# A gate by ScalarE's Silu in place of a tanh and a VectorE product

## The reference

```
g  = jax.nn.silu(xg @ Wg.T)                  # silu(z) = z * sigmoid(z)
...                                          # out: the recurrence over time
og = ((og - m) / jnp.sqrt(va + 1e-05)).reshape(b, l, e) * gn_w + gn_b
x1 = x + og * g @ Wo.T
...
rr = jax.nn.sigmoid(xr2 @ Wfr.T)
kk = jnp.square(jax.nn.relu(xk2 @ Wfk.T))
return x1 + rr * (kk @ Wfv.T)
```

## Time and profile before

| | value |
|---|---|
| median of three executions | 1783.87 us |
| the profiled execution | 1785.44 us |
| its span, first to last instruction | 1783.7 us |
| TensorE busy | 1718.5 us, 96% |
| VectorE busy | 1638.8 us, 92% |
| ScalarE busy | 1184.9 us, 66% |
| GpSimd busy | 955.0 us, 54% |
| mean granted TensorE clock | 0.984 |
| gate's tanh on ScalarE | 32 times, 22.2 us |
| table loads on ScalarE | 5, 1.28 us each |

### The profile page before, as it was taken

One profiled execution on the slowest core, in us unless ns is written; L12 is line 12 of the kernel. 1 busy time (PEld: TensorE's weight loads), 2 busy tenths in 40 slices (PEclk: granted clock), 3 DMA queues, 4 the chain that ended last, 5 costly groups with the idle time before them and its releaser, 6 DMA issues.

```text
span 1783.7 us, 32768 instructions
## 1 busy us (share of the span) xinstructions
PE 1718.5 (96%) x11408; PEld 1218.0 (68%) x11408; DVE 1638.8 (92%) x2224; ACT 1184.9 (66%) x2954; POOL 955.0 (54%) x752
## 2 busy tenths in 40 slices
PE   5899999999999999999999999999999999999876
PEld 3667677677667677766767776776776676776643
DVE  3599999999999999999999999999999999999982
ACT  4666677676677676667767766776766776776533
POOL 1244556556655755555665566565555566545440
PEclk8999999999999999999999999999999999999988
DMA  6243343343343344434334333334433443433320
GB/s 255 71 108 99 96 104 93 105 116 99 96 103 101 91 113 108 101 92 108 92 100 120 99 100 101 99 94 108 114 100 93 106 99 91 115 93 91 104 68 12
DMA packets 81731, 180.81 MB, mean 101 GB/s; under 512 B 18304, under 2 KB 35072, under 8 KB 80544
## 3 DMA queue, kind: packets, MB, share of 16 engines
q1 hardware_dynamic: 59920, 161.93, 34.9%
q10 hardware_dynamic: 21648, 16.78, 3.0%
HBM read 161.91 MB, written 16.78 MB: 100 GB/s over the span
## 4 chain that ended last, share of the span: by engine, by line
PE 84%; DVE 10%; issue 3%; ACT 1%; POOL 1%; DMA 0%; SPq 0%; DVEq 0%; POOLq 0%; ACTq 0%
PE bank L2011 29%; PE bank L2018 17%; PE bank L2135 6%; PE bank L2043 5%; PE bank L2056 5%; PE bank L2023 5%; PE bank L2092 4%; PE bank L2030 3%; DVE S L873 2%; PE bank L2071 2%; DVE A L885 2%; PE bank L2113 1%; PE bank L2146 1%; DVE A L855 1%; PE bank L2036 1%
## 5 line engine op out<-in xcount | busy, mean ns | idle before, releaser
L855 DVE TENSOR_TENSOR A<-vrep,kt 128x1008 f32<-128x1008 f32 x256 | 310.9, 1224 | 2.4
L560 POOL COPY S<-s 128x16 f32<-128x16 f32 x128 | 81.8, 639 | 409.5 <-DVE A L885 409.4
L873 DVE TENSOR_TENSOR_SCAN S<-wrep,S 128x512 f32<-128x512 f32 x256 | 299.8, 1212 | 1.2 <-issue 0.2
L885 DVE TENSOR_TENSOR A<-S,rt 128x2048 f32<-128x2048 f32 x128 | 291.7, 2279 | 0.1
L534 POOL TENSOR_TENSOR xf<-xf,xa 128x512 f32<-128x512 f32 x160 | 223.1, 1395 | 41.3 <-DVE xf L811 41.1
L1496 ACT ACTIVATE bank<-bank,par 128x128 f32<-128x128 f32 x640 | 173.9, 367 | 39.7 <-PE bank L2092 39.2
L503 POOL TENSOR_TENSOR hrs<-hrs,mhalf 128x32 f32<-128x32 f32 x31 | 176.8, 5704 | 2.6
L501 POOL TENSOR_SCALAR rstd<-mv 128x1 f32<-128x1 f32 (+1 forms) x96 | 84.1, 876 | 161.6 <-DVE mv L748 60.8
L552 POOL TENSOR_TENSOR rk<-rT,kT 128x256 f32<-128x256 f32 x32 | 106.0, 3313 | 103.3 <-DVE oc L910 103.3
L863 DVE TENSOR_TENSOR S<-A 128x1008 f32<-128x1008 f32 x128 | 155.8, 1218 | 0.2
L811 DVE TENSOR_TENSOR xf<-bank,sx 128x512 f32<-128x512 f32 x160 | 108.1, 676 | 44.6 <-PE bank L2011 22.5
(11 more groups left out here) (164 smaller groups left out, 4062.1 us busy)
## 6 DMA issues: line engine op xcount, KB each, us to landing
vrep<-v_dram SPq DMA_DIRECT2D x256, 512.0 KB
xc<-x_c SPq DMA_DIRECT2D x32, 256.0 KB, 6.5
xs<-x_s SPq DMA_DIRECT2D x32, 256.0 KB, 7.3
v_dram<-vT ACTq DMA_DIRECT2D x32, 256.0 KB, 3.1
out<-rr ACTq DMA_DIRECT2D x31, 256.0 KB, 2.8
st<-state SPq DMA_DIRECT2D x64, 2.0 KB, 6.6
Wv<-big_w SPq DMA_DIRECT2D x1, 1024.0 KB, 7.7
Wk<-big_w SPq DMA_DIRECT2D x1, 1024.0 KB, 9.4
```

The lines of the kernel that those rows point to most:

```text
L855: ve_.tensor_tensor(A[:, u % 2, half * WJ:(half + 1) * WJ, 0:P - 2], vrep[:, half, :, 0:P - 2], k, ALU.mult).then_inc(dve_outer.sem, 1)
L873: last = ve_.tensor_tensor_scan(s, w, s, 0.0, ALU.mult, ALU.add)
L885: ve_.tensor_tensor(out4, s, r, ALU.mult).then_inc(dve_read.sem, 1)
```

## The change

ScalarE computes silu(z) from bank G with its own Silu function, and mid_gate is dropped from VectorE's lists at all its places. The factor of a half goes out of gnh. Bank G's reader is now ScalarE's step th, and the last item's tail_gate waits for it.

```diff
-        dve_mid = Steps(sem("dve_mid"), "sx xx mv mw mk mr mg s0m s0c g")
+        dve_mid = Steps(sem("dve_mid"), "sx xx mv mw mk mr mg s0m s0c")
...
-  "G": (dve_mid, "g"),
+  "G": (act_mid, "th"),
...
-                po.tensor_scalar(gnh[:, :, :], gn, 0.5, None, ALU.mult).then_inc(pool_const, 1)
+                po.tensor_copy(gnh[:, :, :], gn).then_inc(pool_const, 1)
...
-            def mid_gate(n, m, p):
-
-                eng.wait_ge(act_mid.sem, act_mid.count("th", n))
-                ve_.scalar_tensor_tensor(gT[:, p, :, :], gT[:, p, :, :], 1.0, by_chunk(bank_of("G")[:, :]),
-                                         ALU.add, ALU.mult).then_inc(dve_mid.sem, 1)
...
                 if n == NB - 1:
-                    eng.wait_ge(dve_mid.sem, dve_mid.count("g", n))
+                    eng.wait_ge(act_mid.sem, act_mid.count("th", n))
...
-                mid_gate(*b2)
...
-                sc.activation(gT[:, p, :, :], by_chunk(bank_of("G")[:, :]), ACT.Tanh, scale=0.5).then_inc(act_mid.sem, 1)
+                sc.activation(gT[:, p, :, :], by_chunk(bank_of("G")[:, :]), ACT.Silu).then_inc(act_mid.sem, 1)
```

More of the change, by code:

```diff
@@ L271, in build @@
                   "Tx": (act_mid, "xa"), "W1": (act_mid, "tn"), "Wt": (act_mid, "tx"), "Vp": (act_mid, "vT"), "D1": (act_mid, "dt"),
-                  "D2": (act_mid, "ez"), "E2": (act_mid, "ez"), "Kp": (act_mid, "k"), "Rp": (act_mid, "r"), "G": (dve_mid, "g"),
+                  "D2": (act_mid, "ez"), "E2": (act_mid, "ez"), "Kp": (act_mid, "k"), "Rp": (act_mid, "r"), "G": (act_mid, "th"),
                   "C": (dve_tail, "o1"), "C2": (dve_tail, "o2"), "Tg": (act_tail, "oT"), "Wo": (dve_tail, "x1"),
@@ L1029, in opening @@
                 att_rstd(*at(2))
-                mid_gate(*at(0))
                 mid_shift(*at(1))
@@ L1076, in opening @@
                 att_aggr(*at(3))
-                mid_gate(*at(1))
                 wkv_outer(*at(1), 1)
@@ L1133, in opening @@
                 mid_s0c(*at(2))
-                mid_gate(*at(2))
                 att_rstd(*at(4))
@@ L1264, in closing @@
                 mid_s0c(*at(29))
-                mid_gate(*at(29))
                 wkv_outer(*at(29), 1)
@@ L1325, in closing @@
                 tail_mix(*at(28), 1)
-                mid_gate(*at(30))
                 mid_rw(*at(30))
@@ L1402, in closing @@
                 tail_o2(*at(31))
-                mid_gate(*at(31))
                 tail_ob(*at(31))
```

## The result

The changed kernel takes 1825.3 us (median of four, 1825.03 to 1828.8); the kernel before took 1784.42 beside it. The ratio is 1.0233, 95% interval 1.0215 to 1.0251: 41 us slower. The profiled execution took 1825.03 us, its span is 1823.2.

The account below looks back on a forecast made before the run. TensorE, full in the loop, was taken as the bound: 26 steps x 0.93 = 24.2 us from table loads, less 1.2 and plus 1 for opening and closing, gave +24.0, so 1808 us; range 1788 to 1840.

Parts of the forecast that it names:

- Slower, from table loads: Whole kernel: Silu needs another table than Exp, so each loop step gets two loads; chance of slower 0.83.
- the likeliest case: Loop: loads ahead of the Silu and of rr's tanh, 0.93 us a step, 1808 us in all; chance 0.48.
- first rival: Loop: a load at the first exponential, instead of rr's tanh (1828 us) or at both places (1833 us); chance 0.26.
- TensorE bounds the loop and the product is worth nothing: Loop: TensorE is busy 1360.00 of 1360 us, so removing VectorE's gate product gains 0 in 26 steps.
- The price of a load: ScalarE's burst: one load costs 1.54 us, made of 1.28 load, 0.03 edges and 0.23 lost overlap.
- fourth rival: ScalarE, each of the two table switches in a step: costs 2.66 us in place of 1.54, 1866 us; chance 0.05.
- here I place the load back to the set of Exp and Tanh: ScalarE, loop step: the second load stands ahead of rr's tanh, from 975.24 to 976.52.
- S0 at the place of my forecast: TensorE, loop: the score matmul waiting for Mm starts 0.93 us late with the load back at rr's tanh.
- The matmul on the second normalisation: TensorE, loop: starts at 974.90 in place of 974.21, 0.69 us late, behind the load at the Silu.
- Opening and closing: Outside the loop, six Silus: products off the chain give back 1.2 us, loads cost 1 us (bounds -3 to +8).
- xa is late, but hidden: VectorE, loop: sx starts 0.76 us late behind xa, less than TensorE's own 0.93, so it costs nothing.
- Third rival: ScalarE's waits, loop: loads hide there; both hidden 1784 us, only the first 1804; chance with all hidden 0.05.

Follow-up runs that it names:

- e1: Changed kernel with ScalarE's tanh back in the Silu's place, still without VectorE's product: 1784.65 us against 1784.49 for the kernel before, ratio 1.0001.
- e7: Changed kernel with a one-element Sqrt ahead of the Silu in the 26 loop steps, one more table load in the burst: 1863.32 us, ratio 1.0441.
- e3: Changed kernel with a one-element Exp ahead of the tanh of rr in the 26 loop steps, drawing the load back there: 1804.63 us, ratio 1.0112.
- e2: Kernel before with Silu in place of the gate's tanh and VectorE's product kept: 1827.01 us, ratio 1.0237.
- e5: Changed kernel with one-element Silu ahead of the tail's normalisation and one-element Exp behind the second normalisation, in the loop: 1784.83 us, ratio 1.0002.
- e4: Changed kernel with a one-element Silu ahead of the tail's normalisation in the 26 loop steps, load back left at the first exponential: 1816.2 us, ratio 1.0172.

## Why the prediction was right, and where it was off

**Slower, from table loads: right.** I gave 0.83 to slower and 1788 to 1840 for the range; 1825.3 lies in it. But the likeliest case, 1808, was not the one that came. What came is the first of the first rival's two forms, which I put at 1828; the time lies in the range because its upper end was drawn for that rival. The signs that I named say the same: TensorE waits at line 2030 (2017 in after) but not at 2043 (2030 in after), it waits at 2092 (2079 in after), and the step is 54.10 us, against 53.45 for the forecast and 54.2 for the rival.

**TensorE bounds the loop and the product is worth nothing: right.** e1 measures it: 1.0001. The 1.2 us that I gave back for the opening can't be seen in it. The reason was right for TensorE, but the 0.6 us that I took the product to be worth on VectorE's own line was not: the starts of e1 give some 0.07 in 20 of the 26 steps. The first paragraph also misreads for the opening: there TensorE (134.17 us) is fuller than VectorE (129.68); VectorE is the fuller engine only from 1650 to 1700. The sum doesn't use it.

**The price of a load, 1.54 us in the burst: right.** In after the Silu starts 2.02 us behind its predecessor (985.99 to 988.01), where the tanh started 0.47 behind its own (in the earlier trace rows xa stands 0.48 behind the tanh): 1.55. The 1.46 us a step of e7 are no second measure of it: there the overlap was lost already, and a one-element activation of 0.20 us came with the load. The Trainium skill, "ScalarE: Activation LUTs", section "What ACT_TABLE_LOAD costs", has another 1380 ns of drain, 2.66 us in all, for each switch to another set. Here 0.02 us stand ahead of a load and 0.01 behind it, and e7's whole step grows by 1.46, less than 2.66; the fourth rival (1866) falls with it.

**The step that failed: "here I place the load back to the set of Exp and Tanh".** I put it ahead of rr's tanh, which supposes that Silu's table has no Tanh. No row said so, and the trace of before couldn't show it. My only ground for taking it as the likelier, that otherwise two sets must hold Tanh, came from no row either. After shows the tanh of rr running straight behind the Silu's table with no load (993.42), so the table that Silu loads has Tanh too, and the load moves down to the first Exp. There it meets the matmuls that reuse the exponential's bank. That is the difference of 1808 and 1825: e3 puts the load where I had put it and takes 1804.63, against the 1808 of my sum. The forecast's working for its own place thus held to 3.4 us.

**Terms that were mis-sized.** Two totals are too large by 0.12: S0 at the place of my forecast, 0.93 against 0.81 in e3, and the mixing factors in the first rival, 1.69 against 1.57 in after. Their parts are off by more. The matmul on the second normalisation was 0.69 late by my sum; in after it is 0.33 late, 0.43 with what follows it. From the gate's start to the end of the second normalisation ScalarE took 4.91 us behind the load (988.01 to 992.92) against 5.03 before, and the matmul started 0.05 behind that end where I had charged 0.27. What comes behind it I put too low: 0.24 against 0.35 in e3, and 1.00 against 1.14 in after.

**Opening and closing:** -0.2 by my terms (+1.0 and -1.2), and 40.9 - 41.1 = -0.2 measured. With an interval of 3 us to either side this agreement is luck, and the single terms were not tested. The chain of the opening also holds a third gate product, 0.24 us at 82.59, beside the two that I counted.

**"xa is late, but hidden": right.** VectorE now waits 0.59 us for xa ahead of line 794. In e2 the product itself waits 0.92 us for the Silu, so that sx starts 0.40 us later behind the Silu than in after, and still the step is 54.12 us against 54.10.

**Third rival, loads that hide:** in after neither load of a step stands in a wait; e5 puts both there by hand, and then the loss is gone. Its form with only the first load hidden was priced for a load back at rr (1804); with the load back at the exponential it is e4, 1816.2.

## What to carry to other kernels

Before a function of ScalarE is exchanged, find out which functions share its table, and then follow the list of instructions twice: to the place of the load there and to the first instruction behind it that the new table doesn't hold; in after the load back stood at that one. Price each place by what hangs behind it: a load of 1.28 us cost 0 in a wait, 0.43 where there was room, 1.14 ahead of a bank that TensorE was waiting for, and 1.46, its one-element activation included, where no room was left. A one-element activation of the right function, put where ScalarE waits anyway, moves a load there. The instruction less on VectorE, 92% busy but not the engine that set the pace, was worth nothing; and whether an instruction less shortens its engine's own line at all is to be read from the distance between its neighbours' starts.

## What the runs showed of the hardware

An instruction's recorded duration depends on what stands ahead of it. The Silu behind a load takes 597 ns in all 32 cases, which looks like a gain on the tanh's 710. In e5, where no load stands ahead of it in the loop, the same Silu has a median of 717 ns, and e1's tanh there 712. The lines are of after, e5 and e1 (durations in ns, min/median/max):

```profile
L1544 ACT ACTIVATE gT<-bank x32: 597/597/598, 79.5 to 1773.6; 128x512 f32<-128x512 f32 x32
```
```profile
L1547 ACT ACTIVATE gT<-bank x32: 575/717/723, 80.0 to 1734.3; 128x512 f32<-128x512 f32 x32
```
```profile
L1544 ACT ACTIVATE gT<-bank x32: 577/712/723, 80.4 to 1733.3; 128x512 f32<-128x512 f32 x32
```

The two functions cost the same here. The Trainium skill ("ScalarE: Activation LUTs", section "Step-by-step: what each stage is for") says that of all the functions it tried, per element, and the trace agrees for these two.
